# Last spectral mixing of a four-layer kernel: products of odd and even k in different column groups, two banks for each unit

## The reference, cut to what matters

```python
def _L3_conv_ref(x, weights):
    B, C, H, W = x.shape
    x_f = jnp.fft.rfft2(x)
    k_f = jnp.fft.rfft2(weights)
    out_f = jnp.einsum('bchw,ochw->bohw', x_f, k_f)
    out = jnp.fft.irfft2(out_f, s=(H, W))
    return out
```

## Time and profile before

| | us |
|---|---|
| median of 3 runs | 924.1 |
| the three runs | 920.47, 924.1, 928.2 |
| span of the profiled execution (first to last instruction) | 904.1 |
| median of the runs less that span | 20.0 |
| stage of the mixing within the span | 710.4 to 819.8 |

### The profile page before, as it was taken

The page is one execution under the profiler, slowest core; times in us unless marked ns, Lnnn a source line. Parts: engine busy times, 40 slices in busy tenths (PEclk is TensorE's granted clock), DMA queues, the critical chain, the costliest instruction groups (busy, mean ns, idle before and its releaser), DMA issues. The chain is left out here.

```text
span 904.1 us, 27651 instructions
## 1 busy us (share of the span) xinstructions
PE 755.6 (84%) x11429; PEld 633.2 (70%) x11429; DVE 586.3 (65%) x1097; ACT 456.1 (50%) x768; POOL 86.2 (10%) x80
## 2 busy tenths in 40 slices
PE   7999997785599667876799999958888498988996
PEld 7999996674588546665344444428777388888996
DVE  3554464777847745887786777776666676765445
ACT  0133336775343305652699995007887556775200
POOL 0000000010010002644022313000000100000000
PEclk9999998998899987997999999988999898999998
DMA  8599878862110000000000000004000447860036
GB/s 309 205 344 350 317 217 253 186 137 43 27 31 0 0 2 1 0 0 1 1 1 2 1 1 1 1 1 95 0 0 0 93 95 162 175 128 1 1 142 236
DMA packets 48668, 80.52 MB, mean 89 GB/s; under 512 B 20034, under 2 KB 38472, under 8 KB 43736
## 3 DMA queue, kind: packets, MB, share of 16 engines
q1 hardware_dynamic: 31960, 62.75, 25.0%
q10 hardware_dynamic: 16640, 16.78, 5.4%
HBM read 51.01 MB, written 27.92 MB: 87 GB/s over the span
## 5 line engine op out<-in xcount | busy, mean ns | idle before, releaser
L1588 DVE SCALAR_TENSOR_TENSOR X<-bank,c_power,X 32x512 f32 x128 | 96.8, 756 | 36.5 <-PE bank L1538 32.8
L1731 PE MATMUL bank<-m_xp,m_kf 128*32 128x64 f32 x2048 | 82.7, 248 | 22.2 <-DVE m_xp L1666 11.1
L1731 PEld LDWEIGHTS bank<-m_xp,m_kf 128*32 128x32 f32 x2048 | 81.4, 171 | 23.5 <-issue 23.5
L220 DVE BATCH_NORM_STATS2 bn<-X 128x6 f32 x128 | 83.1, 683 | 2.9 <-POOL X L1328 1.6
L420 DVE COPY ks_rows<-bank 128x512 f32<-128x512 f32 x64 | 41.2, 687 | 66.6 <-PE bank L350 66.6
L438 ACT COPY ks_spec<-bank 128x512 f32<-128x512 f32 x64 | 34.4, 589 | 97.4 <-PE bank L365 97.4
L1494 ACT ACTIVATE c_r<-X,c_nrm 32x1024 f32 (+1 forms) x56 | 74.9, 1337 | 2.4 <-DVE c_nrm L1562 1.1
L350 PE MATMUL bank<-ks_fw,ks_src 64*128 64x64 f32 x1024 | 68.7, 298 | 6.3 <-DMA ks_src<-in_L_conv_weights 6.3
L350 PEld LDWEIGHTS bank<-ks_fw,ks_src 64*128 64x128 f32 x1024 | 68.1, 215 | 6.2 <-issue 6.2
L365 PE MATMUL bank<-ks_fh,ks_rows 64*128 64x128 f32 (+1 forms) x1152 | 71.5, 279 | 0.0
L365 PEld LDWEIGHTS bank<-ks_fh,ks_rows 64*128 64x128 f32 (+1 forms) x1152 | 67.0, 183 | 2.6 <-issue 1.8
(11 more groups left out here) (183 smaller groups left out, 1683.5 us busy)
## 6 DMA issues: line engine op xcount, KB each, us to landing
ks_src<-in_L_conv_weights SPq DMA_DIRECT2D x16, 1024.0 KB, 7.0
kf<-ks_spec ACTq DMA_DIRECT2D x16, 1024.0 KB, 9.2
m_kf<-kf SPq DMA_DIRECT2D x32, 512.0 KB, 8.5
X<-in_x SPq DMA_DIRECT2D x4, 2048.0 KB, 12.6
out_y<-X SPq DMA_DIRECT2D x32, 256.0 KB, 2.6
xf<-l_y SPq DMA_DIRECT2D x24, 112.0 KB, 2.1
l_wb<-in_L_conv_weights_r SPq DMA_DIRECT2D x4, 512.0 KB, 11.5
l_wb<-in_L_conv_weights_i SPq DMA_DIRECT2D x4, 512.0 KB, 13.4
```

The lines of the kernel that those rows point to most:

```text
L220: dve.bn_stats(self.bn[:, c, :], self.X[:, q, c * CH:(c + 1) * CH]).then_inc(step, 1)
L1588: dve.scalar_tensor_tensor(x, of.rearrange("p (y x) -> p y x", x=HN), filt.power[at, 2:3], x, ALU.mult, ALU.add).then_inc(added, 1)
L1731: last = pe.matmul(ps[4 * half + m // 8][at:at + C, m % 8 * N:(m % 8 + 1) * N], kf[p][:, j, :, H * half + m], xp[half][:, j, m].rearrange( ...
```

## The change

The products of a unit go to four column groups: (2 (m % 2) + j), so even and odd k are apart, in place of (2p + j). A unit's results then fill all partitions of two banks (2l and 2l + 1), each unit of a turn having two of its own, and TensorE starts unit n when the read of unit n - 4 is done. ScalarE's read of a unit is still four copies of 64 x 512, now for each parity and bank; it takes 64 partitions of one parity to the 64 of p and writes every second k. The clears have a semaphore each, and TensorE waits for that of xp[0] at l = 0 and of xp[1] at l = 1.

```diff
--- before.py
+++ after.py
@@ -1641,8 +1641,9 @@
     PAIRS = SLOT // 8
     UNITS = 4
     H = N // 2
-    staged, copied, mixed, mixed_read, fix, zeroed = (pr.sem(f"m3_{n}") for n in (
-        "staged", "copied", "mixed", "mixed_read", "fix", "zeroed"))
+    staged, copied, mixed, mixed_read, fix = (pr.sem(f"m3_{n}") for n in (
+        "staged", "copied", "mixed", "mixed_read", "fix"))
+    zeroed = [pr.sem(f"m3_zeroed{p}") for p in range(2)]
     with ExitStack() as ctx:
         kf = [kf0, pr.sb(ctx, "m3_kf1", [P, 2, C, N])]
         xp = [pr.sb(ctx, f"m3_xp{p}", [P, 2, H, 2, 2 * B]) for p in range(2)]
@@ -1677,7 +1678,7 @@
 
             @block.gpsimd
             def _(pool):
-                clear(pool, 0).then_inc(zeroed, 1)
+                clear(pool, 0).then_inc(zeroed[0], 1)
 
             @block.vector
             def _(dve):
@@ -1693,7 +1694,7 @@
 
                 for l in range(UNITS):
                     if l == 1:
-                        clear(dve, 1).then_inc(zeroed, 1)
+                        clear(dve, 1).then_inc(zeroed[1], 1)
                     if l >= 2:
                         dve.wait_ge(mixed, START + l - 1)
                     last = stage(0, l)
@@ -1714,21 +1715,23 @@
             def _(pe):
                 pe.sem_inc(mixed, START)
                 pr.keep_warm(pe, 16)
-                pe.wait_ge(zeroed, 2)
                 with pe.Fori(0, PAIRS) as i:
                     for l in range(UNITS):
                         p, half = l // 2, l % 2
+                        if l < 2:
+                            pe.wait_ge(zeroed[l], 1)
                         if half == 0:
                             pe.wait_ge(loaded[p], 64 * i + 64)
                         pe.wait_ge(staged, UNITS * i + l + 1)
                         pe.wait_ge(copied, UNITS * i + l + 1)
 
-                        pe.wait_ge(mixed_read, START + UNITS * i + l - 1)
+                        pe.wait_ge(mixed_read, START + UNITS * i + l - 3)
                         pe.sem_inc(pr.pace, 1)
                         for m in range(H):
                             for j in range(2):
-                                at = (2 * p + j) * C
-                                last = pe.matmul(ps[4 * half + m // 8][at:at + C, m % 8 * N:(m % 8 + 1) * N],
+                                at = (2 * (m % 2) + j) * C
+                                to = m // 2 % 8 * N
+                                last = pe.matmul(ps[2 * l + m // 16][at:at + C, to:to + N],
                                                  kf[p][:, j, :, H * half + m],
                                                  xp[half][:, j, m].rearrange("p s n -> p (s n)"),
                                                  start=True, stop=True)
@@ -1746,11 +1749,12 @@
                 def read(i, l):
                     act.wait_ge(mixed, START + UNITS * i + l + 1)
                     p, half = l // 2, l % 2
-                    for m in range(4):
-                        at = slice(p * 2 * C, (p + 1) * 2 * C)
-                        k = H * half + 8 * m
-                        c = act.copy(xm[at, bass.ds(2 * i, 2), k:k + 8].rearrange("p s k r b -> p k s (r b)"),
-                                     ps[4 * half + m][at, :].rearrange("p (k s n) -> p k s n", s=2, n=2 * B))
+                    at = slice(p * 2 * C, (p + 1) * 2 * C)
+                    for parity, m in np.ndindex(2, 2):
+                        of = slice(parity * 2 * C, (parity + 1) * 2 * C)
+                        k = H * half + 16 * m + parity
+                        c = act.copy(xm[at, bass.ds(2 * i, 2), k:k + 15:2].rearrange("p s k r b -> p k s (r b)"),
+                                     ps[2 * l + m][of, :].rearrange("p (k s n) -> p k s n", s=2, n=2 * B))
                     c.then_inc(mixed_read, 1)
 
                 for l in range(UNITS):
```

## The result

Slower, where the prediction had faster: a median of 943.8 us (four runs, 933.7 to 947.5) against 925.3 for the kernel before on the same chip (920.5 to 928.2), ratio 1.0177 [1.0114, 1.0241]. The range of 905 to 925 doesn't hold it.

The account below looks back on a forecast made before the run. The last mixing was taken as bound by TensorE and the kf reload in turn. Ending it 14.9 us earlier, less 0.9 for a half-clock stretch, gave a net 14: 924.1 - 14.0 = 910 us, range 905 to 925.

Parts of the forecast that it names:

- the change: a unit on TensorE: Last mixing's products: four column groups take 19.0 ns a record at full clock, so a unit 2.4 or 3.4 us.
- VectorE's staging is unchanged … 4.5 us a unit: Staging of units for the last mixing keeps its 4.5 us and becomes the next limit where no reload waits.
- the no-gain case: Rival at the mixing's products: weight loads stay in line, unit stays 4.9 us, only the head moves; 923.5 us, chance 0.14.
- 33.8 by rows: L770's 16.9 ns a record, doubled because each product uses half the rows; upper bound of 4.3 us a unit.
- The loads as the pace: Reloads of kf in the last mixing set the pace, 10.1 to 10.6 us each, taken as 10.3; chance 0.68, 907 to 915.
- the sum: Last mixing: unit 4 at 744.2, five loads, two last units, 1.0 for a late record; unit 15 ends 14.9 us earlier.
- The rule on packing: Weight loads overlap matmuls only across row groups, so the mixing's units would stay near 4.9 us; treated as a rival.
- Banks, waits, reads, head: Mixing stage: banks, waits and four reads a unit taken as 0; first product starts at 718.6 instead of 723.68.
- The late last record of unit 3: First round of the mixing: a record 3.7 us late may come again and delay the second reload; 1.0 us added.
- The slower one: Rival at L1731: four groups in turn break the overlap, unit 6.9 us, 9 us more, 933; chance 0.05.
- The partly parallel case: Rival at the mixing's products: 33.8 ns a record, unit 4.3 us, 6.8 us less plus 1 from the head, 916; chance 0.13.
- The 20 us outside the span: Median 924.1 us exceeds the profiled span of 904.1 by 20.0, taken as unchanged time before and after the instructions.

Follow-up runs that it names:

- e2: Changed kernel with each product's 32 weights taken side by side in kf (wrong elements) instead of 64 elements apart; 910.3 us, stage 97.1 us.
- e9: Changed kernel with each product's weights 128 elements (512 bytes) apart (wrong elements) instead of 64; stage 126.1 us.
- e10: Changed kernel with weights 65 elements (260 bytes) apart without longer rows (wrong elements); stage 97.5 us.
- e11: Changed kernel with rows of 65 instead of 64 elements in SBUF and HBM, right weights; median 910.9 us against 927.4 for the original kernel.
- e14: Changed kernel with rows of 65 elements, repeated in six runs; 904.5 us against 917.7 for the original kernel, ratio 0.9877.
- e1: Changed kernel with the even k of a unit first, then the odd, so two column groups work at once; 924.8 us, ratio 1.0093 to the original.
- e7: Changed kernel with rows of 68 instead of 64 elements in SBUF and HBM, right weights; median 919.5 us against 919.2 for the original kernel.
- e12: Original kernel, unchanged, executed once more for a second profile; 917.9 us.

## Why the prediction was wrong, step by step

**The step that failed** is "the change: a unit on TensorE", where it takes 19.0 ns a record because "groups stay as independent as two are", together with "VectorE's staging is unchanged … 4.5 us a unit" in the step behind it. Both treat the operand reads as free. L1734's nested windows, columns as in the earlier trace rows:

```profile
753.90:754.40 0.50, 0.50 (x20) 0.50 (x24) 1.00 1.99 262
753.90:757.40 3.50, 3.50 (x128) 3.50 (x128) 1.00 1.04 211
819.00:819.50 0.50, 0.50 (x22) 0.50 (x25) 0.50 0.66 131
819.00:822.50 3.50, 3.50 (x125) 3.50 (x127) 0.50 0.10 19
```

At half clock (125 - 22) / 3.00 us is 29.1 ns a record, at full clock at most 3.00 / 108 = 27.8 ns (the last record of the unit may lie inside the window): the clock hardly matters, where it did in the earlier trace rows (38.0 and 53.6). So something else than the array's clock paces them. Unit 15, with no staging beside it and no DMA (the row 834.20 above), still takes 3.9 us (4.07 at 818.85, with copies beside it), so the copies hardly slow the products; the products stop the copies. With rows of 65 the same 64 products need, on TensorE alone:

```profile
753.00:753.50 0.50, 0.50 (x33) 1.00 1.25 250
753.00:754.50 1.50, 1.50 (x97) 1.00 1.06 211
```

64 records in 1.00 us, 15.6 ns, even less than the 19.0 of the forecast, and 13.9 with the weights side by side (e2); at half clock a unit is 3.65 us (forecast 3.4). What the runs show is that, with four groups at work, reads of weights at 256 and 512 bytes both take longer (a unit of 3.7 us at a granted clock of 1.00 and 0.93, and 2.0 to 2.4 at the other spacings) and all but stop ScalarE's and VectorE's copies. That they meet in the same memory banks is my reading; no run looks into it. The warning stood in the rows: 76 ns for each group where streaming 64 columns needs 53, which I noted and gave to the no-gain case alone, and L1147, my strongest row, has its weights side by side. L770's weights are 128 elements apart, a spacing that stalled here (e9); its "33.8 by rows" was nearer than 19. What stood beside it I never looked up, and it would not have warned me: VectorE's copies of 32x288 (L1420) took 642 to 674 ns beside L770 and 627 and 633 with TensorE idle. So 512 bytes over four groups, with half the rows in each product, stopped nothing there.

The Trainium skill, "SBUF — State Buffer" (section "SBUF: two separate sides"), says "PE, ACT, and DVE's dedicated pair never wait on anyone". The runs disagree for these reads: ScalarE's copy takes 4.62 us beside a unit with 256-byte spacing and 1.07 at most beside one with 260 (e10, e11).

**The loads as the pace** were right, once the weights are read without a stall. e11's timeline on TensorE, then all engines over 751 to 801:

```profile
720.69 3.65 PE L1739 MATMUL bank<-m_xp,m_kf 128*32 128x64 f32 x128 [6.23 <-DVE m_xp L1712]
...
743.52 3.64 PE L1739 MATMUL bank<-m_xp,m_kf 128*32 128x64 f32 x127 [5.06 <-DVE m_xp L1697]
747.82 0.32 PE L1739 MATMUL bank<-m_xp,m_kf 128*32 128x64 f32 x1 [0.65 <-issue]
748.80 3.80 PE L1739 MATMUL bank<-m_xp,m_kf 128*32 128x64 f32 x128 [0.66 <-issue]
...
761.52 6.06 PE L1739 MATMUL bank<-m_xp,m_kf 128*32 128x64 f32 x256 [6.30 <-ACT m_xp L1751]
771.67 5.76 PE L1739 MATMUL bank<-m_xp,m_kf 128*32 128x64 f32 x256 [4.09 <-DMA m_kf<-kf]
781.74 6.17 PE L1739 MATMUL bank<-m_xp,m_kf 128*32 128x64 f32 x256 [4.31 <-DMA m_kf<-kf]
791.86 6.22 PE L1739 MATMUL bank<-m_xp,m_kf 128*32 128x64 f32 x256 [3.95 <-DMA m_kf<-kf]
801.68 6.39 PE L1739 MATMUL bank<-m_xp,m_kf 128*32 128x64 f32 x256 [3.60 <-DMA m_kf<-kf]
```

```profile
751.00:801.00 50.00, 28.06 (x1211) 27.12 (x1203) 42.00 (x97) 40.57 (x58) 0.00 (x0) 0.74 1.00 205
```

Pairs start 10.15, 10.07, 10.12 and 9.82 us apart (forecast 10.1 to 10.6), at a DMA share of 1.00 and 205 GB/s, each after a wait for the reload of some 4 us (forecast 3 to 5). Counted from the stage's start, unit 0 comes at 8.3 us as forecast and unit 14 at 89.3 in place of 85.3: unit 4 starts 2.6 later (748.80), the five loads take 1.4 more. The 2.6 us aren't the reload's but unit 3's, which I had done "by about 740" (29.6 us into the stage) and which ends at 748.1, 35.8 us into it. Its staging was over at 738.8, yet its first product came at 743.52. The profile puts the wait down to VectorE's L1697, whose part for this unit was done; what held it is open. So the sum is right within 4 us for a kernel that I wasn't given: its measured gain is 9 to 13 us in e14 (16.5 by e11's medians) where I had 14.

**The rule on packing** in the Trainium skill, "TensorE: Matmul & The Clock Gate" (section on the mechanism of packing), weighed in the prediction, fell: in e11 every product uses all rows and a record comes every 15.6 ns, a unit in 2.2 us. Nor did it bear the miss: in the changed kernel units got shorter too.

**Banks, waits, reads, head.** Right: 618 ns a read against 598, e1's stage is 2.3 us shorter than before's, and the head is worth 1.5 to 2 us (forecast 2.8 with its faster unit, and less than 1 in the no-gain case, which was too little). The late last record of unit 3 came with 0.65 us in e11 in place of 3.73, but with 5.06 us before the unit's first record; I had added 1.0.

**The rivals.** The slower one (0.05, 933) had the sign and not the mechanism: it put the loss on TensorE, as a unit of 6.9 us. A unit is 3.9; what was broken is its overlap with the staging of the next one, on two engines that the change doesn't touch. The partly parallel case (33.8 ns a record) was near on the rate and missed that as well, at 916.

**The 20 us outside the span** were a misreading: 1.8 us lie outside (947.51 to 945.7, and e1's 925.56 to 923.8). The page of before was of an execution of some 906 us, shorter than the three shown, since its inverse stage ran at full clock almost to its end. That moved no difference, but I took for overhead what is scatter of 20 us in the clock.

## What to carry to other kernels

Before more of TensorE's column groups are set to work at once, look at how far apart the weights' elements lie in a partition. Here, at 256 or 512 bytes, with all 128 rows and four groups, the products were slower and all but stopped many of the copies beside them, and one float32 more in each row took that away. When an engine gets faster, read the longest durations of its neighbours and not the medians: a median of 1044 ns hid copies of 4622. And take the same stage of two executions before calling a gap overhead; a stage that nobody changed varied by 22 us here.

## What the runs showed of the hardware that I had not expected

- Spacing of weights (128 rows, 32 columns, float32, four column groups), with the stage's length, TensorE's time for unit 5 (granted clock 1.00, at 512 bytes 0.93) and the longest ScalarE copy:

| bytes | 4 | 8 | 16 | 64 | 128 | 256 (after) | 260 (e11) | 272 (e7) | 512 |
|---|---|---|---|---|---|---|---|---|---|
| stage, us | 97.1 | 96.7 | 96.9 | 98.0 | 98.3 | 127.8 | 98.2 | 100.0 | 126.1 |
| unit 5, us | 1.99 | 2.00 | 2.22 | 2.17 | 2.37 | 3.75 | 2.25 | 2.24 | 3.68 |
| copy, ns | 1046 | 1047 | 1048 | 1055 | 1055 | 4622 | 1049 | 1046 | 4457 |

- With two column groups 256 bytes cost TensorE some 8 ns a record (38.0 against 30.1) and ScalarE's copies some 60 ns of 1040.
- In the inverse stage the granted clock fell from 1.00 to 0.50 for its last 6 to 56 us (17 profiles), at another time in each execution, in unchanged kernels too, with TensorE busy for 97 to 98% of the stretches before the fall and 85 to 90% behind it (rows 845.00 and 892.80 of after, and those of e12). The stage's length went from 84.3 to 106.6 us with it. What sets the moment is open; no run here tells.
